# A decoder layer on one Trainium2 core: the last batch's two fp32 products as three rounded products each, and other places for splits, norms, rotations and the end

## The chip, the cores and the metric

The kernel runs on one core of one Trainium2 chip. The metric is the device time of one execution in microseconds (us); a kernel's time is the median of its runs.

## The reference

```python
x = x + attention(layernorm(x))            # causal, 16 heads of 32, rotated q and k; y @ w_proj.T at its end
x = x + xattn(layernorm(x), ctx)           # x_m = layernorm(x) @ softmax(energy).T
x = x + ffn(layernorm(x))                  # shared silu expert + top 2 of 8 experts
```

x is (4, 512, 512) in fp32 and ctx (4, 512, 256). In the cross part, query and key come from ctx, the energy is 512x512 for each batch, and its softmax over the last axis multiplies the normed x: this is the mixing of channels. The FFN takes all 2048 tokens: a shared expert of width 704, and eight experts of width 352, of which each token takes two, weighted by the softmax of a router.

## The kernel before

**Batches and places.** Tokens lie on the 128 partitions, 4 tiles (t) of 128 tokens to a batch and 16 tiles for the whole input. Attention runs batch by batch in 64 *places* each. A place holds, for one group of heads and one step of queries, the scores on TensorE (L1178), a masked maximum on VectorE (`probs, mx`, L1552), exp on ScalarE (L877), a transpose on TensorE (L1191), its copy to SBUF on ScalarE (`probsT`, L885) and the weighted sum (L1214), each a place or so behind the one before.

**What fills the places.** All else is inserted into the places by tables of numbers: the projections to q, k and v (L1139, L1164), their rotation (VectorE L1534 to L1544, with one product and one difference on GpSimd, L756 and L762), norm 1 of the next batch (`LN1`, `FIRST_LN1`: statistics, scale L1509, transposes L1080, copies L858, rounding rest `xnT_low` L1606), splits of weights (`SPLIT_WEIGHTS`, `SPLIT_PLACES`), and the cross part of the batch before (`CROSS`; `LAST_CROSS` for the last one): output projection (L1230), context (L1250), energies (L1260) with maximum, exp and division, transposes of the attention (L1271, copies L921), norm 2 with its transposes (L1080, L858), mixing (L1288), norm 3, router (L1297) and the routing on VectorE (L1635 to L1658). The number in a table is `since`, the places since the batch's attention ended. Each engine walks through the places in order and issues what the tables name there, so the order on each engine is fixed at build time.

**The FFN.** From place 260 on (`FFN_PLACE`) shared expert 1 runs. One of its 49 shared places takes two further attention places along, so the last batch's cross part lies inside this loop. A tile's steps are: gate and up on TensorE (L1379), silu on ScalarE (`sg`, L991), its product with up on VectorE (`hidden`, L1837), transposes (L1397), cast `h_hi` (L995), rest `h_lo` (L1841), and nine matmuls of down (L1389). Then come the eight routed experts, each with weights that are split at its start (`gu_hi` L943, `gu_lo` L1703), then shared expert 2 over 16 tiles, and the output DMAs.

**Three rounded products.** A matmul of two fp32 operands is one instruction in the program and two records in the trace. In the other form, both operands are split: ScalarE casts to fp32r (`high`), VectorE subtracts (`low`), and the product is high·high + low·high + high·low, three fp32r matmuls in one accumulation. The QKV projections of batches 1 to 3 and the whole FFN have this form. The output projection (16 matmuls of 128x512 for each batch, 4 tiles by 4 groups g) and the mixing (16 for each batch) are in fp32.

`wp_sb`, the projection's weights, is a slice of a tile that the trace names `attT`; q and k weights are `wqk`.

## Time and profile before

| | us |
|---|---|
| median of 3 runs | 1010.27 |
| lowest, highest | 1008.55, 1011.1 |
| profiled execution | 1009.63 |
| its span | 1007.6 |
| TensorE busy in the span | 964.9 |
| VectorE busy | 617.5 |
| ScalarE busy | 488.5 |
| GpSimd busy | 209.2 |

The span runs from the first to the last instruction of the profiled execution; the 2.0 us between it and that execution's own time lie around it. Busy times overlap, since the engines run side by side. PE is TensorE's matmuls and PEld its weight loads, DVE is VectorE, ACT ScalarE, POOL GpSimd and SP SyncE. Before an instruction an engine may be idle, and the profile names what released it. The granted clock is TensorE's, 1.00 for 2.4 GHz and 0.50 for 1.2 GHz; its mean over the span is 0.993.

### The profile page before, as it was taken

The page shows a single profiled execution, that of the slowest core. Times are in us where ns is not written, and L with a number is a line of the kernel's source. Part 1 is how long each engine was busy: PE and PEld are TensorE (multiplying, and loading weights), DVE is VectorE, ACT ScalarE, POOL GpSimd, SP SyncE. Part 2 cuts the span into 40 slices and gives each one's busy share as a digit, 9 for nine tenths or more (in the row PEclk, how much of TensorE's full clock was granted, in tenths as well). Part 3 has the DMA queues.
Part 4 walks back from the last instruction along what each step waited for, and adds up shares of the span by engine and source line. Part 5 has one row for each costly group of instructions (what it writes and reads, how often), then busy time and mean ns, then how long its engine had stood idle before and what let it go on. Part 6 is the DMA issues. An engine that isn't in the chain of part 4 may idle for free.

```text
span 1007.6 us, 18136 instructions
## 1 busy us (share of the span) xinstructions
PE 964.9 (96%) x6106; PEld 767.1 (76%) x6106; DVE 617.5 (61%) x1625; ACT 488.5 (48%) x1278; POOL 209.2 (21%) x247
## 2 busy tenths in 40 slices
PE   8988899999999999998899999999999999999998
PEld 6457666766767676665667788899889989899997
DVE  5698777867877767768353666524443344434665
ACT  1478765756747566568723331334444344432221
POOL 3222212221112211120000002222232222303342
PEclk9999999999999999999999999999999999999999
DMA  9665854438444473466800211744534542515554
GB/s 242 113 98 74 157 107 64 63 53 244 104 63 64 64 233 65 59 121 206 275 22 21 93 44 53 263 153 166 162 100 140 168 150 85 160 51 157 170 187 144
DMA packets 69834, 124.91 MB, mean 124 GB/s; under 512 B 6336, under 2 KB 22720, under 8 KB 69760
## 3 DMA queue, kind: packets, MB, share of 16 engines
q1 hardware_dynamic: 63296, 104.81, 41.6%
q0 software_dynamic: 5600, 18.35, 6.3%
...
q8 instruction: 43, 0.70, 0.3%
q14 instruction: 31, 0.25, 0.1%
...
## 4 chain that ended last, share of the span: by engine, by line
PE 77%; DVE 11%; issue 3%; DMA 3%; ACT 2%; DVEq 1%; POOL 1%; ACTq 0%; SPq 0%
PE ps L1379 23%; PE ps L1389 12%; PE ps L1139 8%; PE ps L1288 5%; PE ps L1230 5%; PE ps L1191 5%; PE ps L1178 3%; PE ps L1214 3%; PE ps L1164 3%; DVE gu_lo L1703 3%; DMA ks<-rope_a 3%; PE ps L1397 2%; PE ps L1250 2%; PE ps L1080 2%; DVE probs L1552 1%
## 5 line engine op out<-in xcount | busy, mean ns | idle before, releaser
L1552 DVE CUSTOM_DVE_ANT_0 probs<-ps,mask 128x128 f32<-128x128 f32 (+3 forms) x256 | 122.4, 486 | 68.3 <-PE ps L1178 37.6
L885 ACT COPY probsT<-ps 128x128 f32<-128x128 f32 (+3 forms) x256 | 108.7, 426 | 107.6 <-PE ps L1191 66.1
L877 ACT ACTIVATE probs<-probs,nb 128x128 f32<-128x128 f32 (+3 forms) x256 | 146.4, 572 | 24.0 <-DVE nb L1557 23.6
L1178 PE MATMUL ps<-ks,qs 96*128 96x256 f32 (+2 forms) x256 | 128.5, 506 | 13.8 <-DVE mx L1552 10.8
L1191 PE MATMUL ps<-ident,probs 128*128 128x128 f32 x640 | 113.6, 277 | 2.4 <-ACT probsT L885 2.1
L991 ACT ACTIVATE sg<-ps 128x352 f32<-128x352 f32 x69 | 32.1, 465 | 172.5 <-PE ps L1379 172.4
L1837 DVE TENSOR_TENSOR hidden<-sg,ps 128x352 f32<-128x352 f32 x69 | 35.8, 518 | 109.7 <-ACT sg L991 109.7
L1191 PEld LDWEIGHTS ps<-ident,probs 128*128 128x128 f32 x640 | 79.6, 142 | 28.2 <-issue 18.9
L1178 PEld LDWEIGHTS ps<-ks,qs 96*128 96x128 f32 x256 | 49.0, 192 | 51.5 <-DVE mx L1552 23.2
L1389 PE MATMUL ps<-d_hi,h_hi 128*128 128x512 f32 (+1 forms) x207 | 86.8, 419 | 1.3 <-DVE h_lo L1841 1.3
L756 POOL TENSOR_TENSOR rope_a<-rope_a,sin_sb 128x512 f32<-128x512 f32 (+1 forms) x34 | 41.2, 1211 | 225.2 <-DVE rope_a L1534 225.1
L1841 DVE TENSOR_TENSOR h_lo<-ps,h_hi 128x384 fp32r<-128x384 f32 x69 | 38.4, 557 | 72.7 <-ACT h_hi L995 72.6
L1389 PE MATMUL ps<-d_hi,h_lo 128*128 128x512 f32 (+1 forms) x207 | 81.9, 395 | 0.0
L1389 PE MATMUL ps<-d_lo,h_hi 128*128 128x512 f32 (+1 forms) x207 | 81.6, 394 | 0.0
L1379 PE MATMUL ps<-gu_hi,routed_xT_hi 128*128 128x352 f32 x296 | 74.9, 334 | 2.3 <-issue 1.1
L1379 PE MATMUL ps<-gu_hi,routed_xT_lo 128*128 128x352 f32 x296 | 71.5, 323 | 0.0
L1379 PE MATMUL ps<-gu_lo,routed_xT_hi 128*128 128x352 f32 x296 | 71.4, 322 | 0.0
L1379 PE MATMUL ps<-gu_hi,shared_xT_hi 128*128 128x352 f32 x256 | 68.0, 347 | 0.0
L995 ACT CAST h_hi<-ps 128x384 fp32r<-128x384 f32 x69 | 33.3, 483 | 62.7 <-PE ps L1397 62.1
L1379 PE MATMUL ps<-gu_hi,shared_xT_lo 128*128 128x352 f32 x256 | 62.4, 325 | 0.0
L1379 PE MATMUL ps<-gu_lo,shared_xT_hi 128*128 128x352 f32 x256 | 62.3, 325 | 0.0
L762 POOL TENSOR_TENSOR rope_a<-rope_a,rope_b 128x512 fp32r<-128x512 f32 (+1 forms) x34 | 42.6, 1254 | 88.5 <-DVE rope_b L1544 88.5
...
## 6 DMA issues: line engine op xcount, KB each, us to landing
...
```

Of the source, the lines that this page charges most:

```text
L756: nc.gpsimd.tensor_tensor(low, low, sin_sb[:, cols], ALU.mult).then_inc(rope_sine, 1)
L762: nc.gpsimd.tensor_tensor(low.bitcast(F32R), low, high, ALU.subtract).then_inc(rope_done, 1)
L877: nc.scalar.activation(pr, pr, ACT.Exp, bias=nb[:, n % 2, h:h + 1], scale=SCALE, accum_out=sums[:, n % 2, h:h + 1]).then_inc(exp_done, 1)
L885: nc.scalar.copy(probsT[n % 2][:, h, 0:w], ps[:, T_BANK + h % 2, 0:w]).then_inc(pT_done, 1)
L1139: last = nc.tensor.matmul(ps[:, bank, cols], w[:, c, at], xT[:, c, cols], start=(c == 0 and k == 0), stop=(c == CC - 1 and k == len(produc ...
L1178: nc.tensor.matmul(ps[:, S_BANK + h % 2, 0:w], stacks[G % 2][0][:, h, i * P:(i + 1) * P], stacks[G % 2][1][:, h, 0:w], start=True, stop=Tr ...
L1191: last = nc.tensor.transpose(ps[:, T_BANK + h % 2, j * P:(j + 1) * P], probs[n % TT][:, h, j * P:(j + 1) * P], ident[:])
L1230: out_mm = nc.tensor.matmul(ps[:, X_BANK + t % 2, :], yT[:, g, t * P:(t + 1) * P], wp_sb[:, g, :], start=(g == 0), stop=(g == GROUPS - 1))
L1288: last = nc.tensor.matmul(ps[:, X_BANK + t % 2, :], xn_xT[:, t, c, :], attT[:, c, :], start=(c == 0), stop=(c == TT - 1))
L1379: last = nc.tensor.matmul(ps[:, bank, 0:EDIM], xT[:, c, :], w[:, m * CC + c, :], start=(c == 0 and i == 0), stop=(c == CC - 1 and i == 2))
L1389: last = nc.tensor.matmul(ps[:, Y_BANK, :], h[0:fn, f, :], w[0:fn, f, :], start=(f == 0 and i == 0), stop=(f == NF - 1 and i == 2))
L1552: nc.vector.tensor_tensor_reduce(probs[n % TT][:, h, 0:w], ps[:, S_BANK + h % 2, 0:w], mask[:, TOKENS - w:], 1.0, LOWEST, ALU.add, ALU.max ...
```

## The change

1. The last batch's output projection and mixing take the form of three rounded products: 16 + 16 fp32 matmuls become 48 + 48 in fp32r. For this, ScalarE casts the projection's weights (`wp_high`, 4 of 128x512, since 5, 6, 8, 10) and the attention's output (`yT_high`, 4, since 14, 14, 15, 16), and the copies of the turned attention and of the turned norm 2 become casts (`att_high`, `x2T_high`). VectorE subtracts 16 times (`wp_low`, `yT_low`, `att_low`, `x2T_low`, 128x512 each). TensorE now waits for `wp_split` and `y_split` for each group, and for VectorE's `aT_done` and `norm2.copied`, which ScalarE gave before. Tile 0's fourth group is one place later.
2. Places in the tables: the split of `wqk` in batch 0 from place 28 to 18 (`wqk_low` from 30 to 20), norm 1's scales of the first batch later, the transposes, copies and rests of norm 1's tiles 2 and 3 one place later in every batch, the key's rotation of group 15 one place later, and the splits for shared expert 1 from places 54 to 64 of the last batch to 51, 52, 53, 55, 65, 67.
3. The silu table is asked for at shared places 1 (at its end) and 25; the routing's exp comes after the tile's `sg` (table `route_exp`), and the picks after `hidden`.
4. At each expert's start three parts of `gu` are split ahead of silu, product and turn, and the fourth behind.
5. The last tile: transposes into three banks, `h_hi` and `h_lo` in three parts of 128 columns, down in two halves of 256 columns (18 matmuls for 9), the last addition and the output DMA in halves.

```diff
-SPLIT_WEIGHTS = (28, 46, 52, 57, 70, 78)
+SPLIT_WEIGHTS = (18, 46, 52, 57, 70, 78)
...
-OWN_RAW = {1: (5, 8), 2: (0, 5), 3: (0, 7), 4: (49, 55), 10: (2, 7), 15: (1, 5)}
-OWN_SUM = {1: (7, 10), 2: (3, 8), 3: (3, 9), 4: (51, 57), 10: (5, 9), 15: (3, 7)}
+OWN_RAW = {1: (5, 8), 2: (0, 5), 3: (0, 7), 4: (49, 55), 10: (2, 7), 15: (1, 6)}
+OWN_SUM = {1: (7, 10), 2: (3, 8), 3: (3, 9), 4: (51, 57), 10: (5, 9), 15: (3, 8)}
...
-LN1 = dict(stats=(13, 15, 17, 19), variance=(22,), scale=(25, 27, 28, 29), turn=(39, 40, 41, 42), copy=(39, 40, 41, 42),
-           low=(40, 41, 42, 43))
-FIRST_LN1 = dict(LN1, stats=(22, 25, 27, 29), variance=(31,), scale=(33, 34, 35, 36), turn=(40, 41, 42, 43), copy=(40, 41, 42, 43),
-                 low=(41, 42, 43, 44))
+LN1 = dict(stats=(13, 15, 17, 19), variance=(22,), scale=(25, 27, 28, 29), turn=(39, 40, 42, 43), copy=(39, 40, 42, 43),
+           low=(40, 41, 43, 44))
+FIRST_LN1 = dict(LN1, stats=(22, 25, 27, 29), variance=(31,), scale=(34, 36, 37, 38), turn=(40, 41, 43, 44), copy=(40, 41, 43, 44),
+                 low=(41, 42, 44, 45))
...
 CROSS = dict(
+    split_projection=(), split_y=(),
...
-    third_copy=(61, 62, 63, 64), store_mixed=(59,), store=(63,), store_turned=(67,), router=(67,), router_copy=(68,), router_turn=(69,), route=(70, 72, 87))
+    third_copy=(61, 62, 63, 64), store_mixed=(59,), store=(63,), store_turned=(67,), router=(67,), router_copy=(68,), router_turn=(69,), route=(70, 72, 87), route_exp=(70,))
...
-    project=((16, 16, 17, 17), (18, 18, 19, 19), (20, 20, 21, 21), (22, 22, 23, 23)), add_projected=(18, 20, 22, 24),
+    split_projection=(5, 6, 8, 10), split_y=(14, 14, 15, 16),
+    project=((16, 16, 17, 18), (18, 18, 19, 19), (20, 20, 21, 21), (22, 22, 23, 23)), add_projected=(18, 20, 22, 24),
...
-    third_copy=(47, 48, 48, 49), store_mixed=(), router=(50,), router_copy=(50,), router_turn=(52,), route=(52, 53, 54))
+    third_copy=(47, 48, 48, 49), store_mixed=(), router=(50,), router_copy=(51,), router_turn=(52,), route=(53, 55, 56), route_exp=(54,))
...
-        SPLIT_PLACES = tuple((BATCHES - 1) * PLACES + at for at in (54, 56, 58, 60, 62, 64))
+        SPLIT_PLACES = tuple((BATCHES - 1) * PLACES + at for at in (51, 52, 53, 55, 65, 67))
...
+        SILU_PLACES = (1, 25)
+        SOONER = 3
+        LAST_HT_BANKS, LAST_Y_BANKS = (HT_BANK, 4, 6), (Y_BANK, 2)
...
-                    if t == TILES - 1:
-                        sp.wait_ge(shared.y_out, 2 * TILES + 1)
-                    sp.dma_start(out_v[:, t, :], acc[:, t, :]).then_inc(stored, 16)
-            sp.wait_ge(stored, 16 * TILES)
+                    if t < TILES - 1:
+                        sp.dma_start(out_v[:, t, :], acc[:, t, :]).then_inc(stored, 16)
+            for half, cols in enumerate(HALVES):
+                sp.wait_ge(last_out, half + 1)
+                sp.dma_start(out_v[:, TILES - 1, cols], acc[:, TILES - 1, cols]).then_inc(stored, 16)
+            sp.wait_ge(stored, 16 * (TILES + 1))
...
+                    for c in tiles_at(since, 0, when["split_projection"]):
+                        act.wait_ge(wp_loaded, 16 * BATCHES)
+                        act.wait_ge(v_mm, TILES)
+                        nc.scalar.copy(wp_high[:, c, :], wp_sb[:, c, :]).then_inc(wp_made, 1)
+                    for g in tiles_at(since, 0, when["split_y"]):
+                        act.wait_ge(pv_mm, ALL_STEPS)
+                        act.wait_ge(yT_done, p * GROUPS + g + 1)
+                        nc.scalar.copy(yT_high[:, g, :], yT[:, g, :]).then_inc(y_made, 1)
...
                         act.wait_ge(proj_mm, p * TT + TT)
-                        nc.scalar.copy(attT[:, :, t * P:(t + 1) * P],
-                                       ps[:, X_BANK + t % 2, :].rearrange("p (c n) -> p c n", c=TT)).then_inc(aT_done, 1)
+                        dst, done = (att_high, aT_high) if p == BATCHES - 1 else (attT, aT_done)
+                        nc.scalar.copy(dst[:, :, t * P:(t + 1) * P],
+                                       ps[:, X_BANK + t % 2, :].rearrange("p (c n) -> p c n", c=TT)).then_inc(done, 1)
...
                             act.wait_ge(norm1.turned, (p + 2) * TT + t + 1)
-                        copy_turned(norm2, p, t, xn_xT[:, t, :, :], second_bank(p, t))
+                        if p < BATCHES - 1:
+                            copy_turned(norm2, p, t, xn_xT[:, t, :, :], second_bank(p, t), norm2.copied)
+                        else:
+                            copy_turned(norm2, p, t, x2T_high[:, t, :, :], second_bank(p, t), x2_high)
                     for t in tiles_at(since, 0, when["third_copy"]):
-                        copy_turned(norm3, p, t, xn_xT[:, t, :, :], X_BANK + t % 2)
+                        copy_turned(norm3, p, t, xn_xT[:, t, :, :], X_BANK + t % 2, norm3.copied)
...
                         nc.scalar.copy(logits_sb(p), ps[:, X_BANK, :]).then_inc(r_copied, 1)
-                    if since == when["route"][0]:
+                    if since in when["route_exp"]:
...
                     turn(shared, j + 1)
-                    if j == 0:
-                        nc.scalar.activation(silu_unused[:], bias_sb[:, 0:1], ACT.Silu)
...
                     hidden_high(shared, j - 1)
+                if place in SILU_PLACES:
+                    nc.scalar.activation(silu_unused[:], bias_sb[:, 0:1], ACT.Silu)
...
                 act.wait_ge(raw_loaded, (e + 3) * RAW)
-                split(e + 2, e % 2, range(CC))
+                split(e + 2, e % 2, range(SOONER))
...
                 turn(routed, lo + 1)
+                split(e + 2, e % 2, range(SOONER, CC))
...
                     put_routed(total - 1)
-                hidden_high(shared, j)
+                if j < 2 * TILES - 1:
+                    hidden_high(shared, j)
+            act.wait_ge(shared.hT_mm, 2 * TILES)
+            for f in range(NF):
+                nc.scalar.copy(h_hi[:, f, :], ps[:, LAST_HT_BANKS[f], 0:P]).then_inc(last_high, 1)
...
                         pe.wait_ge(wp_loaded, 16 * (p + 1))
-                pe.wait_ge(yT_done, p * GROUPS + g + 1)
-                out_mm = nc.tensor.matmul(ps[:, X_BANK + t % 2, :], yT[:, g, t * P:(t + 1) * P], wp_sb[:, g, :],
-                                          start=(g == 0), stop=(g == GROUPS - 1))
+                if p < BATCHES - 1:
+                    pe.wait_ge(yT_done, p * GROUPS + g + 1)
+                    products = ((yT, wp_sb),)
+                else:
+                    pe.wait_ge(wp_split, g + 1)
+                    pe.wait_ge(y_split, g + 1)
+                    products = ((yT_high, wp_high), (yT_low, wp_high), (yT_high, wp_low))
+                for k, (y, w) in enumerate(products):
+                    out_mm = nc.tensor.matmul(ps[:, X_BANK + t % 2, :], y[:, g, t * P:(t + 1) * P], w[:, g, :],
+                                              start=(g == 0 and k == 0), stop=(g == GROUPS - 1 and k == len(products) - 1))
...
                         pe.wait_ge(xm_added, p * TT + t - 1)
+                products = ((xn_xT, attT),)
+                if p == BATCHES - 1:
+                    products = ((x2T_high, att_high), (x2T_low, att_high), (x2T_high, att_low))
                 for c in chunks:
-                    last = nc.tensor.matmul(ps[:, X_BANK + t % 2, :], xn_xT[:, t, c, :], attT[:, c, :],
-                                            start=(c == 0), stop=(c == TT - 1))
+                    for k, (xT, aT) in enumerate(products):
+                        last = nc.tensor.matmul(ps[:, X_BANK + t % 2, :], xT[:, t, c, :], aT[:, c, :],
+                                                start=(c == 0 and k == 0), stop=(c == TT - 1 and k == len(products) - 1))
...
                     down(shared, j - 1, 1)
-                turn_hidden(shared, j)
+                if j < 2 * TILES - 1:
+                    turn_hidden(shared, j)
+            pe.wait_ge(shared.h_done, 2 * TILES)
+            for f in range(NF):
+                last = nc.tensor.transpose(ps[:, LAST_HT_BANKS[f], 0:P], hidden[:, f * P:(f + 1) * P], ident[:])
+            last.then_inc(shared.hT_mm, 1)
             pe.wait_ge(shared.y_out, 2 * TILES)
-            down(shared, 2 * TILES - 1, 1)
+            for half, cols in enumerate(HALVES):
+                for f, (f0, fn) in enumerate(HCHUNKS):
+                    if half == 0:
+                        pe.wait_ge(last_low, f + 1)
+                    for i, (h, w) in enumerate(((h_hi, d_hi[1]), (h_hi, d_lo[1]), (h_lo, d_hi[1]))):
+                        last = nc.tensor.matmul(ps[:, LAST_Y_BANKS[half], cols], h[0:fn, f, :], w[0:fn, f, cols],
+                                                start=(f == 0 and i == 0), stop=(f == NF - 1 and i == 2))
+                last.then_inc(last_y, 1)
...
+                    for c in tiles_at(since - 1, 0, when["split_projection"]):
+                        dve.wait_ge(wp_made, c + 1)
+                        nc.vector.tensor_tensor(wp_low[:, c, :], wp_sb[:, c, :], wp_high[:, c, :].bitcast(F32), ALU.subtract)\
+                            .then_inc(wp_split, 1)
+                    for g in tiles_at(since, 0, when["split_y"]):
+                        dve.wait_ge(y_made, g + 1)
+                        nc.vector.tensor_tensor(yT_low[:, g, :], yT[:, g, :], yT_high[:, g, :].bitcast(F32), ALU.subtract)\
+                            .then_inc(y_split, 1)
+                    if p == BATCHES - 1:
+                        for t in tiles_at(since, 0, when["attention_copy"]):
+                            dve.wait_ge(aT_high, t + 1)
+                            cols = slice(t * P, (t + 1) * P)
+                            nc.vector.tensor_tensor(att_low[:, :, cols], ps[:, X_BANK + t % 2, :].rearrange("p (c n) -> p c n", c=TT),
+                                                    att_high[:, :, cols].bitcast(F32), ALU.subtract).then_inc(aT_done, 1)
...
                         scale(norm2, p, p, t)
+                    if p == BATCHES - 1:
+                        for t in tiles_at(since, 0, when["second_copy"]):
+                            dve.wait_ge(x2_high, t + 1)
+                            nc.vector.tensor_tensor(x2T_low[:, t, :, :],
+                                                    ps[:, second_bank(p, t), :].rearrange("p (c n) -> p c n", c=CC),
+                                                    x2T_high[:, t, :, :].bitcast(F32), ALU.subtract).then_inc(norm2.copied, 1)
...
-                for i in range(CC):
+                for i in range(SOONER):
...
                 turn(routed, lo + 1)
+                for i in range(SOONER, CC):
+                    low_part(e + 2, e % 2, i)
...
                     add_shared(j - 1)
-                hidden_low(shared, j)
+                if j < 2 * TILES - 1:
+                    hidden_low(shared, j)
+                else:
+                    for f in range(NF):
+                        dve.wait_ge(last_high, f + 1)
+                        nc.vector.tensor_tensor(h_lo[:, f, :], ps[:, LAST_HT_BANKS[f], 0:P], h_hi[:, f, :].bitcast(F32),
+                                                ALU.subtract).then_inc(last_low, 1)
...
             add_picked(TILES - 1)
-            add_shared(2 * TILES - 1)
+            for half, cols in enumerate(HALVES):
+                dve.wait_ge(last_y, half + 1)
+                at = acc[:, TILES - 1, cols]
+                nc.vector.tensor_tensor(at, at, ps[:, LAST_Y_BANKS[half], cols], ALU.add).then_inc(last_out, 1)
```

In the following rows a line's number is followed by the operation, output<-inputs and the shape; x2 is a run of two. Lines are those of each kernel's own file.

**TensorE, the first output projection of the last batch (tile 0).** Before:

```order
L1379 MATMUL ps<-gu_hi,shared_xT_lo 128x352 x2
L1230 MATMUL ps<-attT,yT 128x512 x4
L1389 MATMUL ps<-d_hi,h_hi 128x512
L1389 MATMUL ps<-d_lo,h_hi 128x512
L1389 MATMUL ps<-d_hi,h_lo 128x512
```

and after the change (L1432 is gate and up, L1279 the projection):

```order
L1432 MATMUL ps<-gu_hi,shared_xT_lo 128x352 x2
L1279 MATMUL ps<-wp_high,yT_high 128x512
L1279 MATMUL ps<-wp_high,yT_low 128x512
L1279 MATMUL ps<-wp_low,yT_high 128x512
L1279 MATMUL ps<-wp_high,yT_high 128x512
```

Four fp32 matmuls in one run before the down step are now three groups of three; the fourth group has moved behind the down step and its transposes, where it stands ahead of tile 1's four.

**ScalarE, the routing of the last batch, in the last tiles of shared expert 1.** Before:

```order
L987 CAST shared_xT_hi<-shared_x 128x512
L938 ACT_TABLE_LOAD
L938 ACTIVATE r_sc<-r_t 128x32
L991 ACT_TABLE_LOAD
L991 ACTIVATE sg<-ps 128x352
L995 CAST h_hi<-ps 128x384
L987 CAST shared_xT_hi<-shared_x 128x512
```

and after the change (L975 is the routing's exp, L1028 `sg`, L1070 the unused silu):

```order
L972 COPY attT<-ps 128x512
L1024 CAST shared_xT_hi<-shared_x 128x512
L1028 ACTIVATE sg<-ps 128x352
L975 ACT_TABLE_LOAD
L975 ACTIVATE r_sc<-r_t 128x32
L1032 CAST h_hi<-ps 128x384
L1070 ACT_TABLE_LOAD
L1070 ACTIVATE silu_unused<-bias_sb 128x1
```

The exp and its table load stood ahead of a tile's `sg`, which needed a table load of its own; now `sg` goes first, and the silu table is loaded behind `h_hi`, ahead of the next tile's.

**VectorE, the start of an expert.** Before:

```order
L1703 TENSOR_TENSOR gu_lo<-gu_raw,gu_hi 128x704 x4
L1836 REGISTER_ALU
L1837 TENSOR_TENSOR hidden<-sg,ps 128x352
L1829 REGISTER_ALU
L1832 TENSOR_TENSOR routed_xT_lo<-ps,routed_xT_hi 128x512
L1841 TENSOR_TENSOR h_lo<-ps,h_hi 128x384
L1703 TENSOR_TENSOR d_lo<-d_raw,d_hi 128x1024
```

and after the change (L1788 is the split, L1922 `hidden`):

```order
L1788 TENSOR_TENSOR gu_lo<-gu_raw,gu_hi 128x704 x3
L1921 REGISTER_ALU
L1922 TENSOR_TENSOR hidden<-sg,ps 128x352
L1914 REGISTER_ALU
L1917 TENSOR_TENSOR routed_xT_lo<-ps,routed_xT_hi 128x512
L1788 TENSOR_TENSOR gu_lo<-gu_raw,gu_hi 128x704
L1926 TENSOR_TENSOR h_lo<-ps,h_hi 128x384
L1788 TENSOR_TENSOR d_lo<-d_raw,d_hi 128x1024
```

One of four `gu_lo` has moved from ahead of `hidden` to behind the turned input's rest.

## Rows read from the trace of the kernel before

**Rows 1.** The page of the kernel before, busy times and the chain that ended last.

```profile
PE 964.9 (96%) x6106; PEld 767.1 (76%) x6106; DVE 617.5 (61%) x1625; ACT 488.5 (48%) x1278; POOL 209.2 (21%) x247
...
PE 77%; DVE 11%; issue 3%; DMA 3%; ACT 2%; DVEq 1%; POOL 1%; ACTq 0%; SPq 0%
```

**Rows 2.** What TensorE waited for: engine, line, releaser, us in total, times, longest.

```profile
PE ps L1178 <- DVE mx L1552: 10.8, 16, 2.1
PE ps L1397 <- DVE hidden L1837: 5.7, 11, 1.8
PE ps L1080 <- DVE xnT_low L1606: 3.4, 3, 1.7
...
PE ps L1191 <- ACT probsT L885: 2.1, 2, 1.6
```

**Rows 3.** The chain of waits from 511 to 518 us: start us, us, what.

```profile
511.29 2.09 PE ps L1389 x9
...
513.71 3.44 PE ps L1230 x8
```

**Rows 4.** Four stretches: length, busy us by engine, granted clock (PEclk), DMA share, GB/s.

```profile
73.40:77.40 4.00, 4.00 (x12) 2.05 (x10) 2.70 (x10) 0.87 (x3) 1.50 (x1) 0.57 0.21 57
...
438.80:442.30 3.50, 3.50 (x18) 3.35 (x17) 3.43 (x10) 2.92 (x8) 1.27 (x1) 0.51 0.46 88
...
479.80:483.30 3.50, 3.25 (x9) 1.75 (x9) 1.84 (x4) 3.02 (x10) 0.00 (x0) 0.51 0.83 314
...
585.60:589.10 3.50, 3.50 (x14) 3.50 (x13) 2.41 (x7) 0.75 (x2) 1.86 (x8) 0.51 0.00 0
```

**Rows 5.** Timeline of TensorE: start us, us, instruction [idle before <-releaser].

```profile
72.95 0.39 PE L1178 MATMUL ps<-ks,qs 96*128 96x256 f32 x1 [1.80 <-DVE mx L1552]
...
84.81 0.66 PE L1080 MATMUL ps<-ident,xn_xT 128*128 128x128 f32 x4 [1.67 <-DVE xnT_low L1606]
...
438.12 0.45 PE L1178 MATMUL ps<-ks,qs 96*128 96x384 f32 x1 [2.14 <-DVE mx L1552]
...
478.64 0.41 PE L1191 MATMUL ps<-ident,probs 128*128 128x128 f32 x2 [1.58 <-ACT probsT L885]
...
499.80 0.55 PE L1397 MATMUL ps<-ident,hidden 128*128 128x128 f32 x3 [1.40 <-DVE hidden L1837]
...
584.77 0.44 PE L1397 MATMUL ps<-ident,hidden 128*128 128x128 f32 x2 [1.75 <-DVE hidden L1837]
...
713.21 0.55 PE L1397 MATMUL ps<-ident,hidden 128*128 128x128 f32 x3 [0.27 <-DVE hidden L1837]
```

**Rows 6.** Timeline of VectorE, two scales.

```profile
73.48 0.53 DVE L1509 TENSOR_SCALAR xn_xT<-xn_xT,norm_mv,norm_rstd 128x512 f32<-128x512 f32 x1
...
440.07 1.24 DVE L1509 TENSOR_SCALAR xn<-acc,norm_mv,norm_rstd 128x512 f32<-128x512 f32 x1
```

**Rows 7.** Timeline of GpSimd, two differences of the rotation.

```profile
53.22 1.28 POOL L762 TENSOR_TENSOR rope_a<-rope_a,rope_b 128x512 fp32r<-128x512 f32 x1 [2.60 <-DVE rope_b L1544]
...
439.76 1.27 POOL L762 TENSOR_TENSOR rope_a<-rope_a,rope_b 128x512 fp32r<-128x512 f32 x1 [2.32 <-DVE rope_b L1544]
```

**Rows 8.** Timeline of ScalarE, a cast and a table load.

```profile
476.68 1.06 ACT L943 CAST d_hi<-d_raw 128x1024 fp32r<-128x1024 f32 x1
...
581.98 1.28 ACT L991 ACT_TABLE_LOAD   x1
```

**Rows 9.** Groups of VectorE by line: xcount | busy us, mean ns | idle before.

```profile
L1703 DVE TENSOR_TENSOR gu_lo<-gu_raw,gu_hi 128x704 fp32r<-128x704 f32 x40 | 36.4, 958 | 11.3 <-ACT gu_hi L943 11.3
```

**Rows 10.** Groups from 507 to 550 us, ScalarE copy and VectorE subtraction.

```profile
L1832 DVE TENSOR_TENSOR shared_xT_lo<-shared_x,shared_xT_hi 128x512 fp32r<-128x512 f32 x4 | 2.7, 686 | 2.4 <-ACT shared_xT_hi L987 2.4
...
L921 ACT COPY attT<-ps 128x512 f32<-128x512 f32 x4 | 2.3, 592 | 7.2 <-PE ps L1271 7.2
```

**Rows 11.** Timeline of VectorE at the end of the span.

```profile
1001.44 2.98 DVE L1860 SCALAR_TENSOR_TENSOR acc<-picked,weight,acc 128x512 f32<-128x512 f32 x4
1004.45 0.69 DVE L1850 TENSOR_TENSOR acc<-acc,ps 128x512 f32<-128x512 f32 x1
```

24 lines of the change are left out of this document (21 added, 3 removed).

## Prediction

> **What bounds the kernel now.** I read the page first: TensorE is busy for 964.9 of the span's 1007.6 us, and most of the chain that ended last lies on it [rows 1]. So two things shorten the kernel: less work on TensorE, or less idle time ahead of it. The reader is to see in the next view that the idle time has few owners [rows 2]: scores waiting for the masked maximum, transposes waiting for `hidden`, transposes waiting for `xnT_low`, transposes waiting for a copy on ScalarE. The third view, the chain by its pieces, gives the price of a matmul in either form [rows 3]. The fourth gives stretches in which the granted clock is half, 1.2 instead of 2.4 GHz [rows 4]; there are four, and each stands right behind a stall of 1.5 us or more. The fifth is TensorE's timeline at those stalls [rows 5], and the rest are what the other engines do there [rows 6 to 11]. The sum is made against the profiled execution, 1009.63 us (its span and 2.0 around it); the median of the runs is 0.64 higher, and the forecast is the median less the sum.
>
> **The products.** Eight records, which are four fp32 matmuls of 512 columns, take 3.44 us, so one takes 0.86; nine fp32r matmuls of 512 columns take 2.09, so three take 0.70 [rows 3]. 32 matmuls change form: 32 x 0.16 = **5.2 us less** on the engine that is the bound. The nine run with their weight loads hidden, so I take the low price. The bounds are 0.86 for three (nothing gained) and 0.70.
>
> **The splits that this costs.** ScalarE's copies of the attention and norm 2 become casts of the same shape and cost nothing more; new on it are 8 casts, at most the 0.59 of the copy each [rows 10]. VectorE gets 16 subtractions at 0.69 [rows 10], 11 us in all. Neither engine is the bound in this stretch, so what counts is where TensorE waits for one. Three places have nothing for TensorE ahead of the wait: the first group of tile 0 (`y_split`), the last transposed tile of the attention, and the second pair of norm 2's transposes, whose bank must be read twice before it is free. Each gets one subtraction longer: 3 x 0.69 = **+2.1**. The bounds are 0 (all hidden under gate and up) and all 16 pairs in series (the rival below). The four `wp_low` fall into places where VectorE also owes a maximum, and one comes ahead of `hidden` at the stall of 1.40 at 499.80 [rows 5]; the earlier silu load gives some of it back: **+0.5**, between 0 and 1.3. Cast plus subtraction are the upper end.
>
> **Batch 0 to 1.** Norm 1's transposes waited 1.67 at 84.81 for `xnT_low`, whose place came while VectorE was behind [rows 5]. One place later there is other work ahead: −1.5. The stall of 1.80 at 72.95 is a maximum late on VectorE [rows 5]; the split of `wqk` (a cast on ScalarE and a subtraction on VectorE, each about the 1.06 of the equally large cast [rows 8]) leaves the places ahead of it, but the scales come nearer: −0.4. The stretch at half clock behind it loses 3.5 x 0.49 = 1.7 [rows 4]; I give half a chance that it goes: −0.9. Against that, the subtraction at place 20 now falls beside GpSimd's difference of 1.28 at 53.22 [rows 7]. That such neighbours hurt is seen at 440.07, where a scale that takes 0.53 alone takes 1.24 while GpSimd runs its difference from 439.76 [rows 6, 7]: +0.4, between 0 and 1.28. Together **−2.4**. The Trainium skill, "SBUF — State Buffer", section "Who interferes with whom", states that VectorE and GpSimd share one pair of ports, which one of them holds for a whole instruction, and that a subtraction with both inputs in SBUF takes part in this. By that rule the moved `wqk_low` waits out what is left of GpSimd's, while `att_low` and `x2T_low`, which read one input from PSUM, do not; the trace agrees as far as the scale goes and has no row for such a subtraction beside GpSimd. In the stretch of the last batch's splits GpSimd is nearly idle, so by rule or row nothing is added there.
>
> **Batches 1 to 3, norm 1.** The waits for `xnT_low` are 3.4 in three [rows 2], 1.67 of them the one above; the other two go with the move of tiles 2 and 3: **−1.6**.
>
> **Group 15's keys.** A place later the rotation's product on GpSimd no longer runs beside a scale of norm 2: 1.24 becomes 0.53 [rows 6], −0.7 at the stall of 2.14 at 438.12 [rows 5], and 0.3 of the 1.7 that the half clock behind it costs [rows 4]: **−1.2**. The rest of that stall stays.
>
> **Splits for shared expert 1.** At 478.64 TensorE waited 1.58 for a copy behind the cast of `d`, 1.06 [rows 5, 8]. The last casts move behind place 64: −1.58, and half of the half clock's 1.7 behind it [rows 4]: **−2.4**. The first ones move to places 51 to 53, where GpSimd and VectorE do less.
>
> **Routing and silu.** At 584.77 TensorE waited 1.75 for `hidden` [rows 5], which waited for `sg`, which waited for a table load of 1.28 [rows 8] and the routing's exp ahead of that. Both now come behind `sg`, and the picks behind `hidden`. The table load back to silu comes ahead of the next `sg` with a tile between: −1.75, and 0.8 of the 1.7 at half clock [rows 4]: **−3.1**. The ScalarE instructions are as many as before, and what is late next is the router's tail, for which nobody waits before the experts.
>
> **Expert starts.** Waits for `hidden` are 5.7 in eleven [rows 2]; less the 1.40 and 1.75 of the two above, 2.55 in nine, 0.28 each, as at 713.21 [rows 5]. One `gu_lo` of 0.96 [rows 9] behind `hidden` is more than that: 8 x 0.28 = **−2.3**. It delays `h_lo` by 0.96 at most, with gate and up of the next tile as cover.
>
> **The end.** VectorE adds four picked rows until 1004.42 and then the last 0.69 [rows 11]; the halves can't begin before those four. Only the copy out starts sooner, by half an addition, and its first half is moved then: **−0.1**, between −1.0 and +0.4 (eighteen matmuls of 256 columns for nine of 512).
>
> **Sum.** −5.2 +2.1 +0.5 −2.4 −1.6 −1.2 −2.4 −3.1 −2.3 −0.1 = −15.7. Of the four terms that only move instructions (2.4, 1.6, 1.2, 2.4, together 7.6) I take a third back, 2.5: the instruction that was late is late for someone a place on. That leaves −13.2, and 1010.27 − 13.2 = **997.0** rounded.
>
> **The rivals.**
> - *Moved stalls* (0.25). The four moved terms give nothing and no half clock goes: −5.2 −1.75 −2.3 +2.1 +0.5 −0.1 = −6.75, **1003.5**. For it: the wait for a maximum is 10.8 in sixteen [rows 2], spread over batches, a sign that VectorE is short of time wherever a norm lies. Against: the 1.67 at 84.81 and the 1.58 at 478.64 have one owner each.
> - *All goes* (0.12). No subtraction is exposed and all four half clocks go: −15.7 −2.1, and of the 6.8 for four of them the 3.15 not yet counted: −20.95, **989.3**. For it: each stretch at half clock follows a stall that the change touches. Against: a stall needs only to move to take its stretch with it.
> - *No cheaper* (0.05). Three rounded matmuls with changing weights cost the 0.86 of the fp32 one: −13.2 +5.2 = −8.0, **1002.3**. Against: in [rows 3] the nine change weights too.
> - *Slower: the splits in series* (0.03). TensorE's order is fixed, so each of the 16 splits could hold it for cast and subtraction, 0.59 + 0.69 = 1.28 [rows 10], at the groups of the projection and tiles of the mixing: 20.5. With nothing from the moves: −5.2 −1.75 −2.3 +0.5 −0.1 +20.5 = +11.65, **1021.9**. It decides from 7 exposed of 16. For it: the waits stand there by name. Against: splits run a place or more ahead of their use.
>
> **How the numbers follow.** The forecast has a chance of 0.55; its own range is 993 to 1001 (the products certain to 1, the moves between none and all). The range reaches from the lower rival to past the moved stalls, **989.5 to 1004.5**. A measurement of this kernel can tell 0.3%, 3 us, from no change. Faster by more: 0.55 + 0.25 + 0.12 + 0.05, less 0.03 of the moved stalls that come out smaller still, 0.94. Within 0.3%: 0.03. Slower: 0.03.
>
> **What would show it.** In the profile after: nine matmuls of the projection in 2.1 us, none at 0.86; no wait for `xnT_low`; no wait of over 1 us for `hidden` near 585 and the granted clock whole there; no wait for `hidden` at seven of eight expert starts; waits of about 0.7 for `yT_low`, `att_low` and `x2T_low`, one each. If the granted clock still halves four times, or the wait for the maximum grows from 10.8 by what the others lose, the moved stalls have it. If waits for the three new splits add to over 5 us, the last rival has begun.

## The result, and the profile after

The changed kernel takes **994.44 us** (median of 4, 993.71 to 995.39) beside 1009.41 for the kernel before (4 runs): 15.0 us less, ratio 0.985, 95% interval 0.9832 to 0.9868. The forecast was 997.0, range 989.5 to 1004.5. A second measurement on another chip (`again`, below) gave 995.57 and 0.9868 (0.9853 to 0.9883), which is 13.7 less than the kernel before beside it. So the two measurements give 13.7 and 15.0, and neither interval comes near no change.

The page after: the busy times and the chain, which answer to [rows 1].

```profile
PE 954.6 (96%) x6147; PEld 770.8 (78%) x6147; DVE 624.6 (63%) x1644; ACT 492.1 (50%) x1289; POOL 207.1 (21%) x247
...
PE 80%; DVE 9%; DMA 4%; issue 3%; ACT 3%; POOL 1%; DVEq 0%; ACTq 0%; POOLq 0%
```

TensorE is busy for 10.3 us less, VectorE for 7.1 more: TensorE is still the bound, and the share of VectorE in the chain fell. What TensorE waited for after, which answers to [rows 2]:

```profile
PE ps L1220 <- DVE mx L1617: 7.5, 13, 1.8
PE ps L1450 <- DVE hidden L1922: 2.8, 3, 2.0
...
PE ps L1320 <- DVE att_low L1755: 1.1, 1, 1.1
PE ps L1122 <- DVE x2T_low L1765: 1.0, 1, 1.0
PE ps L1341 <- DVE xnT_low L1671: 1.0, 2, 0.5
...
PE ps L1122 <- DVE xnT_low L1671: 0.8, 1, 0.8
...
PE ps L1279 <- DVE yT_low L1749: 0.7, 1, 0.7
```

The waits for the maximum fell by 3.3, those for `hidden` by 2.9 and from eleven to three; the wait for `xnT_low` went from 3.4 to 0.8, but 1.0 of it now stands ahead of other matmuls (L1341), and the three new splits that TensorE waits for make it wait 1.1, 1.0 and 0.7.

Two of the stalls of [rows 5] are still there. The one of 1.80 at 72.95, which the forecast wanted shorter, is 1.77 at the same maximum, and the one for `hidden` at 499.80 grew from 1.40 to 2.00 (experiment 2).

```profile
72.58 0.39 PE L1220 MATMUL ps<-ks,qs 96*128 96x256 f32 x1 [1.77 <-DVE mx L1617]
```

The chain after, in the stretch of the first output projections, which answers to [rows 3]:

```profile
506.82 2.09 PE ps L1442 x9
508.91 0.49 PE ps L1450 x3
509.39 3.44 PE ps L1279 x15
```

Fifteen rounded matmuls, five products, in the 3.44 us that four fp32 ones took: 0.69 for three beside 0.86.

**Where the 15.7 us between the two profiled spans come from.** Both kernels run the same maxima (L1552, L1617) and the same `sg` in the same order, so the difference of their start times, taken along the program, tells where time was gained (minus: the changed kernel is earlier):

| stretch | us in it | forecast |
|---|---|---|
| start, up to the first maximum | −0.7 | none |
| batch 0, to its place 48 | −0.7 | −2.4 |
| to place 176, norm 1 of batches 2 and 3 within | +0.5 | −1.6 |
| group 15's keys, to place 232 | −1.8 | −1.2 |
| splits for shared expert 1, to the first `sg` | −2.0 | −2.4 |
| projection and mixing, to the seventh `sg` | −2.0 | −2.6 |
| routing, the two next `sg` | −3.5 | −3.1 |
| eight expert starts | −5.1 | −2.3 |
| shared expert 2 and the end | −0.4 | −0.1 |

A half-clock stretch of 1.7 stood in four of these stretches of the kernel before (batch 0, keys, splits, routing) [rows 4], and in none of the changed kernel's; its granted clock is below 1.00 only from 990.5 on, behind its last matmul. If each stretch cost its whole 1.7, then without those 6.8 batch 0 is 1.0 slower, the keys give 0.1, the splits 0.3 and the routing 1.8; the splits' stretch holds the new casts of the weights too. How much of the 6.8 belongs to the change is asked below, and there (experiments 8 and 12) such a stretch is seen to cost less than 1.7. The +0.5 up to place 176 isn't the change's either: this profile loses 0.5 between places 144 and 148, and `again`, the same program, doesn't. The forecast's column adds up to −15.7; the 2.5 that it took back are not in it.

### The profile page after: what moved, and what is told of

Same layout as the page of the kernel before. It is cut to its first block, busy times and chain, and to the rows that moved or that the text cites. A ratio compares the mean times of both kernels' runs of the same rounds, so it can differ in the third digit from the quotient of the medians.

```text
span 991.9 us, 18270 instructions
## 1 busy us (share of the span) xinstructions
PE 954.6 (96%) x6147; PEld 770.8 (78%) x6147; DVE 624.6 (63%) x1644; ACT 492.1 (50%) x1289; POOL 207.1 (21%) x247
## 4 chain that ended last, share of the span: by engine, by line
PE 80%; DVE 9%; DMA 4%; issue 3%; ACT 3%; POOL 1%; DVEq 0%; ACTq 0%; POOLq 0%
PE ps L1432 26%; PE ps L1442 14%; PE ps L1181 8%; PE ps L1341 5%; PE ps L1279 5%; PE ps L1233 5%; PE ps L1220 3%; DMA ks<-rope_a 3%; PE ps L1256 3%; PE ps L1206 3%; PE ps L1450 2%; PE ps L1420 2%; PE ps L1122 1%; DVE probs L1617 1%; DMA qs<-rope_b 1%
## 5 line engine op out<-in xcount | busy, mean ns | idle before, releaser
L1617 DVE CUSTOM_DVE_ANT_0 probs<-ps,mask 128x128 f32<-128x128 f32 (+3 forms) x256 | 122.3, 486 | 64.6 <-PE ps L1220 32.9
L1028 ACT ACTIVATE sg<-ps 128x352 f32<-128x352 f32 x69 | 32.0, 464 | 159.8 <-PE ps L1432 158.3
L1922 DVE TENSOR_TENSOR hidden<-sg,ps 128x352 f32<-128x352 f32 x69 | 35.8, 519 | 95.7 <-ACT sg L1028 95.7
L1442 PE MATMUL ps<-d_hi,h_hi 128*128 128x512 f32 (+1 forms) x204 | 84.0, 412 | 0.0
L1432 PE MATMUL ps<-gu_hi,routed_xT_hi 128*128 128x352 f32 x296 | 74.7, 334 | 1.9 <-issue 1.1
L1432 PE MATMUL ps<-gu_hi,routed_xT_lo 128*128 128x352 f32 x296 | 71.5, 323 | 0.0
L1432 PE MATMUL ps<-gu_lo,routed_xT_hi 128*128 128x352 f32 x296 | 71.5, 323 | 0.0
L1432 PE MATMUL ps<-gu_hi,shared_xT_hi 128*128 128x352 f32 x256 | 65.4, 337 | 0.0
L1432 PE MATMUL ps<-gu_lo,shared_xT_hi 128*128 128x352 f32 x256 | 61.8, 323 | 0.0
L1432 PE MATMUL ps<-gu_hi,shared_xT_lo 128*128 128x352 f32 x256 | 61.8, 322 | 0.0
```

The source lines that it names most:

```text
L1432: last = nc.tensor.matmul(ps[:, bank, 0:EDIM], xT[:, c, :], w[:, m * CC + c, :], start=(c == 0 and i == 0), stop=(c == CC - 1 and i == 2))
L1442: last = nc.tensor.matmul(ps[:, Y_BANK, :], h[0:fn, f, :], w[0:fn, f, :], start=(f == 0 and i == 0), stop=(f == NF - 1 and i == 2))
L1617: nc.vector.tensor_tensor_reduce(probs[n % TT][:, h, 0:w], ps[:, S_BANK + h % 2, 0:w], mask[:, TOKENS - w:], 1.0, LOWEST, ALU.add, ALU.max ...
```

## The experiments

All are edits of the changed kernel and compared with its 994.44 or, by their traces, with it place by place. Three groups of four ran on three chips; the medians of the kernel before there were 1009.08, 1008.72 and 1009.24. The changed kernel's own two medians, 994.44 and 995.57, lie 1.1 apart, so differences of medians of about 1 us tell nothing by themselves. Where a trace shows the difference place by place, it counts for more, and it is taken against `again` too.

**1. The products in fp32.**

```diff
-    split_projection=(5, 6, 8, 10), split_y=(14, 14, 15, 16),
+    split_projection=(), split_y=(),
...
-    if p < BATCHES - 1:
+    if True:
...
-    if p == BATCHES - 1:
+    if False:
```

(and the casts become copies, the subtractions go.)

> The changed kernel with the last batch's projection and mixing in fp32 again, without the 8 casts and 16 subtractions; all moves stay. Theory 1 (the forecast's terms): the rounded form gave 5.2 us and cost about 2.6 in waits, so this kernel is about 2.6 slower than the changed one, near 997.0, and its last-batch stretch shows 0.86 for each projection matmul. Rival (three rounded cost what one fp32 does): it saves the waits and loses nothing, near 991.8. Rival (the gain was in the half clock): within 1 us of the changed kernel, or with a half-clock stretch of 3.5 us back in this stretch, 1.7 more.

997.05 (996.21 to 998.3), 2.6 slower than 994.44 and 1.5 slower than 995.57; by the traces it loses 2.0 between the first and the seventh `sg`, with the clock whole in both. Its chain in the projection:

```profile
509.78 4.29 PE ps L1276 x10
```

Ten records, five matmuls, 0.86 each. Theory 1 holds: three rounded products are cheaper (0.69 beside 0.86 is 5.5 for 32). Of these 5.5, 2.0 are left by the traces, so nearly two thirds go back into waits.

**2. No low parts.**

```diff
-    ((yT_high, wp_high), (yT_low, wp_high), (yT_high, wp_low))
+    ((yT_high, wp_high), (yT_high, wp_high), (yT_high, wp_high))
```

(and so for the mixing; the 16 subtractions are left out and TensorE waits for the casts.)

> The changed kernel without the 16 subtractions: all three products take the rounded (high) parts, so the low parts are left out of the last batch's projection and mixing. Theory 1: the subtractions stand in TensorE's way at three places and ahead of hidden at one: 2.1 + 0.6 = 2.7 faster than the changed kernel, near 991.7. Rival: TensorE then waits for ScalarE's casts at the same places, at most 0.5 faster, near 994. Rival (splits in series): over 8 us faster.

990.73 (990.53 to 991.96), 3.7 faster; by the traces 3.2 within the stretch from the first `sg` to the fifth. Theory 1 in kind, but the subtractions cost 3.2 there and not 2.6. The changed kernel's TensorE and VectorE show where: `wp_low` stands between a maximum and `hidden`,

```profile
494.59 0.68 DVE L1745 TENSOR_TENSOR wp_low<-attT,wp_high 128x512 fp32r<-128x512 f32 x1
495.19 0.51 DVE L1922 TENSOR_TENSOR hidden<-sg,ps 128x352 f32<-128x352 f32 x1
```

and TensorE's idle time ahead of the transposes that follow, and ahead of those that need a bank again:

```profile
495.76 0.55 PE L1450 MATMUL ps<-ident,hidden 128*128 128x128 f32 x3 [2.00 <-DVE hidden L1922]
...
528.95 0.63 PE L1320 MATMUL ps<-ident,xn 128*128 128x128 f32 x4 [1.05 <-DVE att_low L1755]
...
535.83 1.25 PE L1122 MATMUL ps<-ident,xn 128*128 128x128 f32 x8 [1.02 <-DVE x2T_low L1765]
```

The same transposes in this kernel, where only the casts are left to wait for:

```profile
495.25 0.55 PE L1450 MATMUL ps<-ident,hidden 128*128 128x128 f32 x3 [1.40 <-DVE hidden L1922]
...
526.63 0.63 PE L1320 MATMUL ps<-ident,xn 128*128 128x128 f32 x4 [0.33 <-ACT att_high L955]
...
532.78 1.14 PE L1122 MATMUL ps<-ident,xn 128*128 128x128 f32 x8 [0.29 <-ACT x2T_high L883]
```

and in the kernel before, where the same banks were copied:

```profile
533.83 0.63 PE L1271 MATMUL ps<-ident,xn 128*128 128x128 f32 x4 [0.33 <-ACT attT L921]
...
539.98 1.14 PE L1080 MATMUL ps<-ident,xn 128*128 128x128 f32 x8 [0.29 <-ACT xn_xT L858]
```

So the cast's part, 0.33 and 0.29, was there before the change, and each subtraction adds 0.60 to 0.73 by the brackets: 0.60 ahead of `hidden`, 0.72, 0.73, and 0.69 at tile 0's third group for `yT_low`. Together that is 2.7. The rest up to 3.2 shows in the distances between starts. Tile 0's third group starts 1.08 after the matmul ahead of it, where 0.23 will do, so this wait costs 0.85 and not 0.69:

```profile
504.81 0.39 PE L1279 MATMUL ps<-wp_low,yT_high 128*128 128x512 f32 x1
505.89 0.47 PE L1279 MATMUL ps<-wp_high,yT_high 128*128 128x512 f32 x1 [0.69 <-DVE yT_low L1749]
```

**3. Four parts ahead at each expert's start.**

```diff
-        SOONER = 3
+        SOONER = CC
```

> The changed kernel with all four parts of gu split ahead of hidden at each expert's start, as before. Theory 1 (the forecast's term): only the 0.28 us of wait for hidden at each of 8 starts comes back, 2.3, near 996.7. Theory 2 (after the two traces): a start costs 0.7, since gate and up of the next tile also wait for the low part of its turned input, which stands behind hidden on VectorE: 8 x 0.7 = 5.6, near 1000. Rival: nothing, within 1 us.

999.67 (999.2 to 1000.85), 5.2 slower: theory 2. By the traces it loses 5.6 over the experts, at seven of the eight starts (the first shows none): 0.7 to 0.8 at each but one, and 1.1 at the one shown here. This kernel's TensorE at the start that [rows 5] show at 713.21:

```profile
702.75 0.40 PE L1442 MATMUL ps<-d_hi,h_lo 96*128 96x512 f32 x1
703.72 0.55 PE L1450 MATMUL ps<-ident,hidden 128*128 128x128 f32 x3 [0.57 <-DVE hidden L1922]
704.32 0.59 PE L1432 MATMUL ps<-gu_hi,routed_xT_hi 128*128 128x352 f32 x2
```

and its VectorE:

```profile
699.52 3.71 DVE L1788 TENSOR_TENSOR gu_lo<-gu_raw,gu_hi 128x704 fp32r<-128x704 f32 x4 [1.58 <-ACT gu_hi L980]
703.16 0.51 DVE L1922 TENSOR_TENSOR hidden<-sg,ps 128x352 f32<-128x352 f32 x1
703.59 0.68 DVE L1917 TENSOR_TENSOR routed_xT_lo<-ps,routed_xT_hi 128x512 fp32r<-128x512 f32 x1
```

The changed kernel's TensorE at the same start:

```profile
701.92 0.40 PE L1442 MATMUL ps<-d_hi,h_lo 96*128 96x512 f32 x1
702.16 0.49 PE L1450 MATMUL ps<-ident,hidden 128*128 128x128 f32 x3
702.41 0.56 PE L1432 MATMUL ps<-gu_hi,routed_xT_hi 128*128 128x352 f32 x2
```

There are two waits, not one. The first, for `hidden`, has a bracket of 0.57, and the transposes start 0.97 after the matmul ahead of them where 0.24 will do. After `hidden` TensorE transposes and then needs the low part, which VectorE ends at 704.27: gate and up begin at 704.32, 0.60 after the transposes and not 0.25. The second wait has no bracket in the view, since the transposes' modelled ends reach into it; only the distance between starts shows it.

**4. The routing ahead of `sg`.**

```diff
-    router_copy=(51,), router_turn=(52,), route=(53, 55, 56), route_exp=(54,))
+    router_copy=(50,), router_turn=(52,), route=(52, 53, 54), route_exp=(52,))
...
-        SILU_PLACES = (1, 25)
+        SILU_PLACES = (1,)
```

> The changed kernel with the routing's exp and picks ahead of the tile's sg and hidden again, and one early silu load only. Theory 1: the stall of 1.9 comes back near 574 and with it a stretch of 3.5 us at half clock, 1.7: together 3.6, near 998.0. Rival (the clock doesn't follow the stall): 1.9, near 996.3, granted clock whole. Rival (the stall moves elsewhere): within 1 us.

996.89 (996.58 to 997.64), 2.4 slower; by the traces 1.9 at this place. TensorE there:

```profile
579.12 0.55 PE L1450 MATMUL ps<-ident,hidden 128*128 128x128 f32 x3 [1.74 <-DVE hidden L1922]
```

and the stretches of this kernel behind two stalls, at 73.5 and at 579.5 (columns as in [rows 4]):

```profile
73.50:77.00 3.50, 3.50 (x9) 1.67 (x8) 1.35 (x6) 0.71 (x3) 1.26 (x1) 0.53 0.32 73
...
579.50:583.00 3.50, 3.50 (x24) 3.50 (x23) 2.78 (x9) 1.00 (x2) 1.86 (x8) 1.00 0.00 0
```

The stall came back whole and its half clock did not. Yet the stall near 72, which this edit doesn't touch, had a half clock behind it here and none in the changed kernel's profile. So the rival holds in this execution, and one stall doesn't decide the clock.

**5. Norm 1 at its old places.**

```diff
-LN1 = dict(..., turn=(39, 40, 42, 43), copy=(39, 40, 42, 43), low=(40, 41, 43, 44))
+LN1 = dict(..., turn=(39, 40, 41, 42), copy=(39, 40, 41, 42), low=(40, 41, 42, 43))
```

(and `FIRST_LN1` with its scales.)

> The changed kernel with norm 1's scales, transposes, copies and rests at their places of before. Theory 1 (the forecast's terms): 1.5 at batch 0's and 1.6 at the two later ones come back, 3.1, near 997.5. Theory 2 (after the two traces, where the same maxima in batches 1 to 3 come no sooner): the later two give nothing, only batch 0's comes back, 0.5 to 1.5, near 995.4.

995.63 (993.89 to 997.02), with clocks of 0.996 to 0.999. Its waits for `xnT_low` are back,

```profile
PE ps L1122 <- DVE xnT_low L1671: 3.4, 3, 1.7
```

but its maxima are hardly later: counted from the first maximum it is level with the changed kernel at place 48, and at place 176 it is 0.4 ahead of it and 0.2 behind `again`. Moving norm 1 is worth 0.1 to 0.2 at most, and nothing at batch 0: the 1.67 at 84.81 [rows 5] became two waits that this view of the changed kernel's TensorE shows, and others like them.

```profile
83.42 0.66 PE L1122 MATMUL ps<-ident,xn_xT 128*128 128x128 f32 x4 [0.79 <-DVE xnT_low L1671]
...
88.20 0.50 PE L1181 MATMUL ps<-xnT_high,wqk_high 128*128 128x512 f32 x1 [0.46 <-DVE xnT_low L1671]
```

**6. The split of wqk at place 28 and group 15's keys a place earlier.**

```diff
-SPLIT_WEIGHTS = (18, 46, 52, 57, 70, 78)
+SPLIT_WEIGHTS = (28, 46, 52, 57, 70, 78)
...
-OWN_RAW = {..., 15: (1, 6)}
-OWN_SUM = {..., 15: (3, 8)}
+OWN_RAW = {..., 15: (1, 5)}
+OWN_SUM = {..., 15: (3, 7)}
```

> The changed kernel with the split of wqk at place 28 and group 15's keys a place earlier, as before. Theory 1 (the forecast's terms): the split's move is worth 0 to 0.4 and the half clock's chance there, the keys 1.2; 1.2 to 2.5 slower, near 996.3. Theory 2 (after the two traces): between the maxima of places 0 and 24 the split's move costs 0.8, and the keys give 1.8, so the net is 1.0. Told apart by the times of the maxima: at place 24 this kernel is 0.8 ahead of the changed one, at place 236 1.0 behind it.

997.45 (997.05 to 997.77), clocks 0.994 to 0.996. By the maxima, counted from the first, it is 1.0 ahead of the changed kernel at place 24, but only 0.5 from place 36 to 144. At place 148 it is 1.0 ahead again, and that half is the 0.5 that the changed kernel's profile loses there; of `again` it is 0.5 ahead. The keys cost it 1.7 up to place 232, of which 1.1 is given back four places on: 0.7 net. So the split's new place costs 1.0 at first (theory 2) and 0.5 for good, and the keys' move is worth 0.7 and not 1.8.

The traces show what the split's new place does on VectorE. The subtraction beside GpSimd's difference, in the changed kernel:

```profile
52.60 1.28 POOL L787 TENSOR_TENSOR rope_a<-rope_a,rope_b 128x512 fp32r<-128x512 f32 x1 [2.60 <-DVE rope_b L1609]
...
53.35 1.60 DVE L1587 TENSOR_TENSOR wqk_low<-wqk,wqk_high 128x1024 fp32r<-128x1024 f32 x1
```

and at its old place in the kernel before, with GpSimd idle:

```profile
66.97 1.22 DVE L1522 TENSOR_TENSOR wqk_low<-wqk,wqk_high 128x1024 fp32r<-128x1024 f32 x1
```

The neighbour costs 0.38, which is the forecast's +0.4. The rest is the subtraction's own 1.22, which now stands ahead of the maximum of place 21.

**7. The split alone at place 28** (`SPLIT_WEIGHTS` as in 6).

> The changed kernel with only the split of wqk back at place 28. Theory (from the maxima of wqk_keys_back, 1.0 ahead at place 24 and not behind later by as much): 0.5 to 1.0 faster than the changed kernel. Rival (the forecast's term, a gain of 0.4 and a half clock): 0.5 to 1.3 slower.

995.69 (993.94 to 996.03), the same as 995.57 of `again` beside it. In its profile it is 0.9 ahead at place 24 and has lost 1.8 by place 36, where the stretch from 74 runs at half clock. What the move costs in waits it may save in clock; with these spreads that stays open.

**8. The splits for shared expert 1 at their old places.**

```diff
-        SPLIT_PLACES = ... (51, 52, 53, 55, 65, 67))
+        SPLIT_PLACES = ... (54, 56, 58, 60, 62, 64))
```

> The changed kernel with the splits for shared expert 1 at places 54 to 64 of the last batch, as before. Theory 1 (the forecast's term): the copy waits for the cast again, 1.6, with a half clock in some executions, near 996.5. Theory 2 (after the two traces): 1.3, since another wait, for the scaled norm, stands a place further on in the changed kernel. Rival: nothing.

999.28 (998.62 to 1000.33), 4.8 slower, with clocks of 0.994 and 0.995 in all four. TensorE:

```profile
477.49 0.41 PE L1233 MATMUL ps<-ident,probs 128*128 128x128 f32 x2 [1.58 <-ACT probsT L910]
478.50 0.63 PE L1122 MATMUL ps<-ident,xn 128*128 128x128 f32 x4 [0.59 <-DVE xn L1574]
```

These are the old waits, but the 1.58 is not what the move gains: the changed kernel waits 0.63 for the same copy and 0.99 for norm 2's scale. What is gone lies ahead: two waits for a maximum, 0.83 and 0.24, and most of one for norm 2's scale, 0.73 to 0.16. The traces put 1.3 between places 248 and 252, before the 1.58, 0.4 up to the last maximum and 1.1 up to the first `sg`, of these 1.7 for the stretch from 480 at half clock. So the move is worth 1.1 if that stretch costs its whole 1.7 (theory 2 said 1.3, by another wait). But `again` has such a stretch from 475.7 and lost only 0.8 to the changed kernel up to the first `sg`: at half clock TensorE comes later to what it waits for, and waits less. Its TensorE, and the changed kernel's:

```profile
476.51 3.29 PE L1299 MATMUL ps<-ctx_sb,wq_sb 128*128 128x512 f32 x4 [0.31 <-ACT xn_xT L883]
...
483.22 0.66 PE L1358 MATMUL ps<-ident,xn 128*128 128x128 f32 x4 [0.34 <-ACT xn L972]
```

```profile
477.07 1.98 PE L1299 MATMUL ps<-ctx_sb,wq_sb 128*128 128x512 f32 x4 [0.46 <-ACT xn_xT L883]
...
482.98 0.66 PE L1358 MATMUL ps<-ident,xn 128*128 128x128 f32 x4 [0.85 <-ACT xn L972]
```

From place 240 on the move is worth 1.8 against `again`. So it is worth 1.1 to 1.8. The medians' 4.8 is not all its own: this kernel's clock is the lowest of the changed ones, and one of its three stretches stands at 74, which the edit doesn't touch.

**9. Turns and weight casts spread out.**

```diff
-    split_projection=(5, 6, 8, 10), ...
+    split_projection=(4, 5, 6, 8), ...
...
-    attention_turn=(25, 26, 27, 27), ... second_turn=(30, 30, 31, 31), second_copy=(30, 31, 31, 32),
+    attention_turn=(25, 26, 27, 28), ... second_turn=(29, 30, 31, 32), second_copy=(29, 30, 31, 32),
```

> The changed kernel with the casts of the projection's weights at since 4, 5, 6, 8 for 5, 6, 8, 10 and the turns of attention and norm 2 one tile to a place. Theory: wp_low no longer stands ahead of hidden (0.6), and TensorE has gate and up between a tile's turn and the next that needs its bank (1.05 and 1.02 of waits for att_low and x2T_low): 2.7 faster than the changed kernel, near 991.8. Rival: the waits move with the turns, within 1 us.

995.45 (992.47 to 996.85), not told from the changed kernel. By its trace, which is that of its fastest execution, it takes 1.1 less from the first `sg` to the fifth, not 2.7. The 0.6 for `hidden` came. Of the two banks' waits most went to the first turn of norm 2, now too near its scale:

```profile
531.67 0.63 PE L1122 MATMUL ps<-ident,xn 128*128 128x128 f32 x4 [1.95 <-DVE xn L1574]
```

**10. The same with norm 2's first two turns at 30, and wqk's split at 28.**

> The changed kernel with three edits: the casts of the projection's weights at since 4, 5, 6, 8; the turns of the attention one tile to a place, and norm 2's third and fourth at 31 and 32; the split of wqk at place 28. Theory: 0.6 for hidden, 1.05 and 1.0 for the two banks, 0.5 to 1.0 for wqk: 3 faster than the changed kernel. Rival (as in spread, the waits move on to the scaled norm): 1 to 1.5 faster.

994.53 (993.12 to 998.66) beside 995.57: not told from the changed kernel, and by its trace 0.3 less from the first `sg` to the fifth. Neither its theory nor its rival came: the wait moved again, to four waits for `hidden`, 3.8, where the changed kernel has three and 2.8. So none of my versions beats it by what can be measured.

```profile
PE ps L1450 <- DVE hidden L1922: 3.8, 4, 1.5
```

**11. The old end.** One bank, one cast, one rest, nine matmuls, one addition, one DMA.

> The changed kernel with the end of before: last tile's transposes into one bank, one cast, one rest, nine matmuls of 512 columns, one addition, one output DMA. Theory (the forecast's term): 0.1 slower, VectorE's four additions of picked rows set the end. Rival (after the two traces: from the last sg to the end of the span the changed kernel takes less): 0.3 to 0.6 slower.

995.85 (994.12 to 996.34), not told from 995.57. From the last `sg` to the end of the span the profiles say more: 9.58 us here and in the kernel before, 9.42 in the changed one, 9.41 in `again`. The new end gives 0.2. The additions of the picked rows start 3.32 behind the last `sg` in the changed kernel and 3.40 here; the rest of the gain lies behind them. The changed kernel:

```profile
985.67 0.36 PE L1548 MATMUL ps<-d_hi,h_hi 128*128 128x256 f32 x1 [0.77 <-DVE h_lo L2041]
985.84 2.98 DVE L1945 SCALAR_TENSOR_TENSOR acc<-picked,weight,acc 128x512 f32<-128x512 f32 x4
```

**12. The changed kernel again.**

> The changed kernel itself, unaltered, beside the kernel before on one chip. Theory: of the 15 us about 3.5 are fewer stretches at half clock, of which each takes 0.0017 from the mean granted clock and costs 1.7 us; so over the executions the mean clock is about 0.9955 before and 0.999 here, and 994.4 is measured again. Rival: the clock differs from chip to chip and not by kernel; here it is then as low as before's, and the difference is 11 to 12 us, near 997.5.

995.57 (995.5 to 996.11); mean clocks 0.996 to 0.997, and 0.993 to 0.997 for the kernel before beside it. Two stretches of this execution's profile, the first a stall and the second right behind it:

```profile
493.80:495.90 2.10, 0.21 (x1) 0.00 (x0) 1.82 (x4) 0.34 (x1) 0.00 (x0) 1.00 0.93 263
496.00:499.40 3.40, 3.39 (x52) 2.88 (x56) 0.00 (x0) 2.39 (x5) 0.00 (x0) 0.54 0.03 8
```

The same program's first profile, the same stall:

```profile
493.80:495.70 1.90, 0.00 (x0) 0.00 (x0) 1.87 (x4) 0.09 (x1) 0.00 (x0) 1.00 1.08 317
495.80:499.50 3.70, 3.70 (x69) 3.33 (x70) 0.29 (x1) 3.02 (x6) 0.00 (x0) 1.00 0.16 41
```

So a stall of 2 us is followed by half clock in some executions and not in others. (In `again` an earlier stretch, from 475.7, was at half clock too.) Over 23 executions of the kernel before, in these three groups, the mean clock is 0.9953, over 8 of the changed one 0.9978; a stretch takes 0.0017. That is 2.8 stretches against 1.3, and 0.0025 of the span, **2.5 us**, for the change; 6.8 in the pair of profiles was the luck of one execution with four and one with none. Even the 2.5 is rough: on the one chip that ran both together, the means are 0.9952 and 0.9968, which is 1.5 us, the low clock behind the last matmul takes up to 0.0007 off a mean and costs nothing, and a stretch was seen to cost 0.8 to 1.6 where its 1.7 was expected (experiment 8; 1.6 at 73.4 in `route_first`). Neither theory nor rival holds as written: clocks differ between groups, and the changed kernel's is still the higher one beside the kernel before.

## Why the prediction was right

The time fell within the range, 2.6 below the forecast; the gain was forecast at 13.2 and measured at 13.7 to 15.0. But errors of opposite sign met.

- **Products**, −5.2: right; 0.69 for 0.86 is −5.5.
- **Splits in the way**, +2.1 and +0.5: right in kind and place (`att_low`, `x2T_low`, `wp_low` ahead of `hidden`, and `yT_low` in tile 0, though at its third group and not its first), a little low in size: `no_low` gives 3.2 to 3.7. One subtraction for each place was right by the brackets, 0.60 to 0.73 each, 2.7 in all; the earlier silu load gave nothing back (`no_low` waits 1.40 for `hidden`, like the kernel before); the 1.05 and 1.02 hold 0.33 and 0.29 that the kernel before waited already. What the forecast lacks shows only between starts.
- **Expert starts**, −2.3: the term that failed most, 5.1 between the kernels before and after, 5.2 to 5.6 by `four_ahead`. The step "2.55 in nine, 0.28 each" read the wait from the list of waits; the second wait, for the low part of the turned input behind `hidden`, isn't in it, and the first one's bracket is short. A start costs 0.7 to 0.8, at seven of eight.
- **Batch 0**, −2.4, and **norm 1**, −1.6: wrong. "There is other work ahead" was argued and not costed; `norm1_back` shows the waits with their old sizes and hardly later maxima; in the changed kernel TensorE waits 0.79 and 0.46 a little further on. The stall of 1.80 at 72.95, from which −0.4 was to come, is still 1.77. The rival *moved stalls* had this right for these two terms. The +0.4 for GpSimd's part in `wqk_low` was right (1.60 beside it, 1.22 alone); what the sum put at nothing is the subtraction's own 1.22 ahead of a maximum. The move costs 1.0 at place 24 and 0.5 later.
- **Keys**, −1.2 of which −0.7 without clock: 0.7 by `wqk_keys_back`. The pair of profiles gives 0.1, with its stretch taken at the whole 1.7.
- **Splits for shared expert 1**, −2.4, of which −1.58 without clock: 1.1 to 1.8, and mostly not where I had put it, at the copy behind the cast, but at the three waits ahead of it.
- **Routing**, −1.75 and 0.8 of 1.7: the stall is right (1.9 by `route_first`), and no run shows that its clock goes with it.
- **End**, −0.1: 0.2.
- **The third taken back**, +2.5: without the clock's 2.25 the four moved terms were 5.35, with the discount 2.85. The versions that undo them show 0.7 for the keys, 1.1 to 1.8 for the splits, about nothing for norm 1 and −0.5 to −1.0 for wqk: 0.8 to 2.0. The discount was too small.
- **Half clock.** The shares I gave (0.9, 0.5, 0.85, 1.4) make 3.65; the means give 1.5 to 2.5. That they would go with their stalls was wrong as a mechanism: in the changed kernel's profile a stall of 1.77 and one of 2.00 have whole clock behind them.

So the moves were overrated by 0.8 to 2.0, the clock by 1.1 to 2.1, and the cost of the splits was underrated by 0.6 to 1.1, while the expert starts were underrated by 2.8 to 3.3 and the products, the routing and the end by 0.5 together. From 13.2 that makes 11.3 to 14.5, and 13.7 to 15.0 were measured. That the total came out within 2 us is partly luck: errors of 2 to 3 us of opposite sign met. Whether the edits help or hinder each other stays open, since they were undone one or two at a time.
